# A three-layer graph network on one core: clears and edge work moved behind the first layer's loads, tiles loaded ahead of weight rows, a second weight buffer, an earlier read of the branch register

## What is computed

```python
deg = segment_sum(ones, dst);  deg_inv = 1 / max(deg, 1)
def sage(h, W_self, W_neigh, b):
    mean = segment_sum(h[src], dst) * deg_inv[:, None]
    return h @ W_self + mean @ W_neigh + b
h   = relu(sage(x, W_self0, W_neigh0, b0))
x   = layernorm(x + sage(h, W_self1, W_neigh1, b1))
g   = x @ W.T + b
d   = deg_of_src_with_self_loops ** -0.5
out = layernorm(x + segment_sum(d[row] * d[col] * g[col], row))   # edges and self loops
```

## Time and profile before

| | |
|---|---|
| three timed executions | 949.64, 946.65, 945.94 us, median 946.65 us |
| the profiled execution | 954.31 us, its span 952.6 us |
| PE matmul busy | 880.7 us, 92% of the span |
| PE weight load, DVE, ACT, POOL busy | 747.3, 383.1, 144.4, 411.7 us |
| chain of work that ended last | PE 81%, DMA 7%, DVE 5% |
| mean granted TensorE clock | 0.965 |

### The profile page before, as it was taken

One profiled execution on the slowest core, in us unless ns is written; L12 is line 12 of the kernel. 1 busy time (PEld: TensorE's weight loads), 2 busy tenths in 40 slices (PEclk: granted clock), 3 DMA queues, 4 the chain that ended last, 5 costly groups with the idle time before them and its releaser, 6 DMA issues.

```text
span 952.6 us, 11246 instructions
## 1 busy us (share of the span) xinstructions
PE 880.7 (92%) x4403; PEld 747.3 (78%) x4403; DVE 383.1 (40%) x683; ACT 144.4 (15%) x200; POOL 411.7 (43%) x335
## 2 busy tenths in 40 slices
PE   4749998799997999979997899999999999999996
PEld 3538887688897888968886688888888989988885
DVE  3284667100003676721114122223665643445554
ACT  3101113101102211220104000001111222210000
POOL 3038878877778687786777882000000000000000
PEclk9679999899997999989999799999999999999999
DMA  8926864546376788543347477886656666755551
GB/s 299 383 69 211 306 199 126 164 108 182 100 210 176 188 274 272 161 123 90 90 113 265 146 259 235 276 273 195 198 165 216 202 214 195 270 188 180 200 207 66
DMA packets 109818, 185.56 MB, mean 195 GB/s; under 512 B 16398, under 2 KB 85014, under 8 KB 103616
## 3 DMA queue, kind: packets, MB, share of 16 engines
q1 hardware_dynamic: 58320, 113.56, 36.8%
q10 hardware_dynamic: 40208, 69.37, 20.1%
q0 software_dynamic: 11232, 1.84, 3.5%
HBM read 114.83 MB, written 69.69 MB: 194 GB/s over the span
## 4 chain that ended last, share of the span: by engine, by line
PE 81%; DMA 7%; DVE 5%; another core or an unknown queue 2%; issue 2%; ACT 1%; POOL 0%; ACTq 0%; SPq 0%; DVEq 0%; POOLq 0%
PE ps L1134 41%; PE ps L1209 10%; PE ps L1222 9%; PE ps L1157 9%; PE ps L1189 9%; DMA u<-edges_scr 4%; DMA xs<-xt_scr 2%; PE ps L1120 1%; DVE w L760 1%; PE ps L1178 1%; PE ps L1090 1%; PE ps L1080 1%; ACT outb L631 1%; DVE repeat L825 1%
## 5 line engine op out<-in xcount | busy, mean ns | idle before, releaser
L1134 PE MATMUL ps<-w,xs 128*128 128x512 f32 x1440 | 348.0, 403 | 41.2 <-ACT w L578 16.4
L1134 PEld LDWEIGHTS ps<-w,xs 128*128 128x128 f32 x1440 | 278.6, 195 | 103.0 <-ACT w L578 18.7
L513 POOL DMA_INDIRECT adj_in<-mult,idx_in x160 | 199.5, 1247 | 96.4 <-issue 96.4
L513 POOL DMA_INDIRECT adj_out<-loops,idx_out x160 | 200.8, 1255 | 68.6 <-issue 61.8
L1157 PE MATMUL ps<-xs,w 128*128 128x512 f32 (+1 forms) x576 | 113.6, 358 | 9.2 <-DMA xs<-xt_scr 8.2
L1157 PEld LDWEIGHTS ps<-xs,w 128*128 128x128 f32 x576 | 96.9, 191 | 26.2 <-DMA xs<-xt_scr 8.6
L1189 PE MATMUL ps<-w,u 128*128 128x256 f32 (+3 forms) x640 | 99.3, 314 | 1.2 <-issue 0.9
L1134 PE MATMUL ps<-u,xs 128*128 128x512 f32 x432 | 98.2, 389 | 0.0
L1189 PEld LDWEIGHTS ps<-w,u 128*128 128x128 f32 (+1 forms) x640 | 90.0, 194 | 9.1 <-issue 2.2
L1134 PEld LDWEIGHTS ps<-u,xs 128*128 128x128 f32 x432 | 81.0, 188 | 16.8
L1209 PE MATMUL ps<-u,xs 128*128 128x512 f32 (+1 forms) x400 | 91.3, 390 | 0.2 <-issue 0.2
(11 more groups left out here) (128 smaller groups left out, 581.3 us busy)
## 6 DMA issues: line engine op xcount, KB each, us to landing
xs<-xt_scr SPq DMA_DIRECT2D x30, 1024.0 KB
xt_scr<-xs ACTq DMA_DIRECT2D x10, 1024.0 KB
xin<-in_x SPq DMA_DIRECT2D x18, 512.0 KB
xs<-xt_scr SPq DMA_DIRECT2D x16, 512.0 KB
adj_in<-u ACTq DMA_DIRECT2D x4, 1600.0 KB, 20.9
adj_out<-u ACTq DMA_DIRECT2D x4, 1600.0 KB
w<-adj_in SPq DMA_DIRECT2D x5, 1280.0 KB, 8.1
xs<-adj_in SPq DMA_DIRECT2D x10, 640.0 KB, 5.4
```

Of the source, the lines that this page charges most:

```text
L513: pool.indirect_dma_start(table, bass.IndirectOffsetOnAxis(ap=index[0:EP, j:j + 1], axis=0), counts[0:EP, j:j + 1], None, bounds_check=CEL ...
L1134: ins = nc.tensor.matmul(acc[:, cols], xs[:, t % 2, k, left * T:(left + 1) * T], w_row(q, k, right)[:, cols], start=(i == 0), stop=(i == l ...
```

## The change

The change has six parts. (a) ACT issues the four zero transfers into `adj_in` after all eight splits of N0's weights, not after four. (b) DVE's edge work in N0 is spread: `edge_cells` and `edge_form` move one tile later, `repeats` two tiles later or more, the last two behind S0's splits. (c) PE turns the next tile of x after 4 steps of a tile instead of 16, except in tile 0, and N0's first step waits for the high part of x alone. (d) In S0 and S1, SP issues the first tiles' loads ahead of weight rows 4 to 7. (e) N1 and GCN use a second raw weight buffer (the first 1024 columns of `key`), and the square root of `dsum` moves from the end of mean0 to block 27 of 32. (f) PE reads the flag register after `linear(N0, 3)`; bank 6 comes first in S0's block order.

```diff
-    BLOCK_ORDER = (4, 5, 6, 7, 0, 1, 2, 3)
+    BLOCK_ORDER = (6, 4, 5, 7, 0, 1, 2, 3)
...
-        raw_slots = [raw[:, 0, :], raw[:, 1, :], outb[:, 0, :], outb[:, 1, :]]
+        raw_slots = [raw[:, 0, :], raw[:, 1, :], outb[:, 0, :], outb[:, 1, :], key[:, :, :].rearrange("p g c -> p (g c)")[:, 0:D]]
...
-                raw_slot[l, k] = 0 if l in (N1, GCN) else k % 2 if l == "wt" else k % 4
+                raw_slot[l, k] = k % 2 * 4 if l in (N1, GCN) else k % 2 if l == "wt" else k % 4
...
@@ SP, ahead of S0 @@
-            for k in range(KD):
+            for k in range(4):
                 sp.wait_ge(w_lo_done, KD * S0 + k - 3)
                 load_w(S0, k)
             for i, (c, k) in enumerate(S0_STEPS):
                 t0, n = CHUNKS0[c]
+                if i == 2:
+                    for row in range(4, KD):
+                        sp.wait_ge(w_lo_done, KD * S0 + row - 3)
+                        load_w(S0, row)
...
@@ SP, mean0 @@
-                if m in (0, 4, 8, 12, 16, 28):
-                    k = min(m // 4, 5)
-                    sp.wait_ge(w_lo_done, KD * N1 + k)
+                if m in (0, 1, 4, 8, 12, 16, 30):
+                    k = {0: 0, 1: 1, 4: 2, 8: 3, 12: 4, 16: 5, 30: 6}[m]
+                    if k == 1:
+                        sp.wait_ge(batch_ready, GROUPS)
+                    elif k >= 2:
+                        sp.wait_ge(w_lo_done, KD * N1 + k - 1)
                     load_w(N1, k)
...
-            for k in (6, 7):
-                sp.wait_ge(w_lo_done, KD * N1 + k)
-                load_w(N1, k)
+            sp.wait_ge(w_lo_done, KD * N1 + 6)
+            load_w(N1, 7)
...
@@ SP, ahead of S1 @@
-            for k in range(KD):
-                if k < 4:
-                    sp.wait_ge(w_lo_done, KD * (N1 + 1))
-                else:
-                    sp.wait_ge(w_lo_done, KD * S1 + k - 3)
+            for k in range(4):
+                sp.wait_ge(w_lo_done, KD * (N1 + 1))
                 load_w(S1, k)
...
             for t in range(NT):
                 sp.wait_ge(acc_full, acc_index(S1, t - 2) + 1)
                 load_tile(t)
+                if t == 0:
+                    for k in range(4, KD):
+                        sp.wait_ge(w_lo_done, KD * S1 + k - 3)
+                        load_w(S1, k)
...
@@ SP, gather @@
             load_w(GCN, 0)
+            load_w(GCN, 1)
...
-                for k in {1: (1, 2), 2: (3, 4), 3: (5,)}[c]:
-                    sp.wait_ge(w_lo_done, KD * GCN + k)
+                for k in {1: (2, 3), 2: (4, 5), 3: (6,)}[c]:
+                    sp.wait_ge(w_lo_done, KD * GCN + k - 1)
                     load_w(GCN, k)
...
@@ ACT @@
             for k in range(KD):
                 split_hi(N0, k)
-                if k == 3:
-                    clear(adj_in, cleared_in)
+            clear(adj_in, cleared_in)
             store_turned(0)
...
+                if m == 27:
+                    act.wait_ge(dscale_step, 1)
+                    nc.scalar.activation(dsqrt[:, :], dsum[:, :], ACT.Sqrt).then_inc(dsqrt_done, 1)
             store_h(31)
-            act.wait_ge(dscale_step, 1)
-            nc.scalar.activation(dsqrt[:, :], dsum[:, :], ACT.Sqrt).then_inc(dsqrt_done, 1)
...
@@ DVE, N0 @@
                     turn_lo(t + 1)
                     if t == 0:
                         edge_keys()
+                    elif t == 1:
                         edge_cells()
                     evict_lo(N0, t)
-                    if t == 0:
+                    if t == 1:
                         edge_form()
                         repeats(0)
                         dve.wait_ge(b0_turned, 1)
                         nc.vector.tensor_copy(b0c[:, :], ps[:, 7, 0:KD]).then_inc(b0c_ready, 1)
-                    repeats(t + 1)
+                    elif t >= 2:
+                        repeats(t - 1)
...
+            for g in range(NT - 2, GROUPS):
+                repeats(g)
...
@@ PE @@
                 if q == N0:
-                    pe.wait_ge(xt_lo_done, t + 1)
+                    pe.wait_ge(xt_hi_done, t + 1)
...
-                    if q == N0 and t < NT - 1 and i == 16:
+                    if q == N0 and t < NT - 1 and i == (16 if t == 0 else 4):
                         turn_tile(t + 1)
...
+                    if q == N0 and (k, left) == (0, 1):
+                        pe.wait_ge(xt_lo_done, t + 1)
...
             for t in range(NT):
                 linear(N0, t)
+                if t == 3:
+                    pe.wait_ge(flag_ready, 2)
+                    general = pe.value_load(flag[0:1, 0:1], min_val=0, max_val=1)
...
             self_turned()
-            general = pe.value_load(flag[0:1, 0:1], min_val=0, max_val=1)
             with pe.If(general > 0):
```

More of the change, by code:

```diff
@@ L197, in build @@
         x_full = sems("x_full", 2)
-        raw_full = sems("raw_full", 4)
+        raw_full = sems("raw_full", 5)
         xt_stored = sems("xt_stored", 2)
@@ L264, in build @@
         weights = [w_neigh0, w_self0, w_neigh1, w_self1, wt_scr]
-        raw_slot, raw_count, loads = {}, {}, [0] * 4
+        raw_slot, raw_count, loads = {}, {}, [0] * 5
         for l in (N0, S0, N1, S1, "wt", GCN):
             for k in range(KD):
-                raw_slot[l, k] = 0 if l in (N1, GCN) else k % 2 if l == "wt" else k % 4
+                raw_slot[l, k] = k % 2 * 4 if l in (N1, GCN) else k % 2 if l == "wt" else k % 4
                 loads[raw_slot[l, k]] += 1
@@ L476, in _ @@
                 if t == 1:
-                    for k in (6, 7):
-                        sp.wait_ge(w_lo_done, KD * GCN + k)
-                        load_w(GCN, k)
+                    sp.wait_ge(w_lo_done, KD * GCN + 6)
+                    load_w(GCN, 7)
                     for j in range(4):
@@ L943, in _ @@
                     dve.wait_ge(dsum_done, done)
+                    if done == NT // 2:
+                        nc.vector.tensor_scalar(dsum[:, :], dsum[:, :], 1.0, None, ALU.add).then_inc(dscale_step, 1)
                 if d == 5:
@@ L949, in _ @@
             h_rest(31)
-            nc.vector.tensor_scalar(dsum[:, :], dsum[:, :], 1.0, None, ALU.add).then_inc(dscale_step, 1)
             split_lo(N1, 6)
@@ L1153, in self_turned @@
                             pe.wait_ge(acc_free, acc_index(N0, 8 + d // 2) + 1)
-                        elif first and d == 6:
-                            pe.wait_ge(flag_ready, 2)
                         for left, right in ((0, 0), (0, 1), (1, 0)):
```

## The result

| | before | after |
|---|---|---|
| median of four timed executions | 947.31 us (945.94 to 949.64) | 903.37 us (902.75 to 904.90) |
| ratio after / before | | 0.9522, 95% interval 0.9504 to 0.954 |
| the profiled execution, its span | 954.31, 952.6 us | 903.53, 901.8 us |
| mean granted TensorE clock | 0.965 | 0.985 |
| PE matmul busy | 880.7 us, 92% | 869.2 us, 96% |

The kernel became 44 us faster. That is 18 us short of the 885 us forecast, and above the range's upper end of 900. The waits of PE show where: total us, times, longest, as in the earlier trace rows.

What follows compares the result with a forecast made beforehand. PE is busy nearly throughout, so time returns only from its waits (five hold 56.1 us) and the half clock behind them. Savings of 61.2 us take the profiled 954.3 to 893.1, less 7.7 gives 885 us; range 877 to 900.

Steps and rivals of the forecast that it cites:

- the offset: Whole kernel: the median of timed runs lies 7.7 us below the profiled execution, taking 893.1 to 885 us.
- N0, wait and clock: N0's first tiles: tile 2 starts at 40.5 instead of 66.94, saving 26.4 us of wait and 3.0 of half clock.
- S0, wait: Start of S0: first pieces of x issued one tile earlier remove the wait, 8.1 us.
- S0, clock: Behind S0's first wait: the half clock goes with the wait, 1.9 us.
- wait in front of mean0: Branch to mean0: the early register read gives 2 us of lead, 2.0 us saved, bounds 0.7 and 4.4.
- N1 and S1: First tiles of N1 and S1: waits of 4.8 and 9.8 us go, each with 2.6 us of half clock.
- The rate of 0.22 MB/us: SP's queue beside POOL's before the zeros: three weight rows take 7.1 us, row 7 cast at 22.5.
- rival 1: N0: edge windows land at 45.3, PE waits 11.4 us in tile 1 plus 2.5 of half clock; 899 us, chance 0.17.
- the limit of 33.9: N0, tile 1: windows must land by 33.9 for PE not to wait; expected at 28.5, margin 5.4 us.
- Rival 2: Waits form again one transfer later, as at S0's piece 2 with 2.6 us of margin; 892 us, chance 0.13.
- rival 3: Front of mean0: the moved read gives only its own 0.7 us, the fetch being the wait; 886.5 us, chance 0.2.
- rival 4: mean0: POOL's puts become the bound, each us of start after 70 costing one; 890 us at 75, chance 0.05.

Runs made afterwards that it cites:

- fourth kernel: Changed kernel with tile 0's store ahead of the zeros, zeros paired behind stores of tiles 1 and 2, POOL's windows held until weight row 6 is cast: 902.53 us.
- the fastest kernel: The fourth kernel with zeros behind the stores of tiles 2 and 3, and the other zeros, edge work, `bad` and register read later: 887.38 us.
- twelfth kernel: Changed kernel with the register read back in front of the branch, bank 6 still first: 904.79 us.
- fifth kernel: Changed kernel with the load of mean0's second group of panels moved from the end of S0 to block 4 of mean0: 901.58 us.
- the tenth: The fastest kernel with the load of mean0's second panels held until PE's first matmuls of mean0 are done, ahead of block 4: 889.07 us.

## Why the prediction missed, step by step

The miss has two parts. In the profiled executions the change saved 50.8 us where the sum had 61.2: 10.4 us, and the step that failed is N0's. The other 7.7 us are the offset: I took the profiled execution of before to stand above its median for good. Four medians of that kernel in the study lie between 947.3 and 949.3, and its profiled 954.3 lies above every timed execution (the highest 952.5), while the changed kernel's profiled 903.5 is at its median. The offset belonged to one execution and should have been taken as a bound. The timed executions show 44 us saved, so some 7 of the 50.8 us in the table are this one execution's and not the change's; in which rows they lie isn't shown.

| | predicted | measured |
|---|---|---|
| N0, wait and clock | 29.4 | 14.4 (end at 149.0 against 163.4) |
| S0, wait | 8.1 | 8.1 |
| S0, clock | 1.9 | 2.9 (the stage's length, 111.9 against 114.7) |
| wait in front of mean0 | 2.0 | 2.1 |
| length of mean0 | 0 | 3.3 |
| N1 and S1 | 19.8 | 20.1 |
| sum | 61.2 | 50.8 (954.31 - 903.53; the terms are rounded) |

**N0, the step that failed.** The prediction put row 7 at 22.5, tile 1's start at 28.0, tile 2's at 40.5. The runs gave 27.15, 33.15 and 52.29. Three things are in the 15.0 us:
1. *The store of tile 0*, listed as "(0.3)" of issuing behind the zeros. I costed its instruction and not its landing, and did not ask who waits for it: `store_turned(0)` frees the half of `xs` for the cast of tile 2. The order in the front part shows it directly behind the four transfers. Its landing at 51.1 costs 4.2 us of wait and 3.2 of half clock; moving it alone gave 7.4.
2. *Row 7*, 4.7 us late. The rate of 0.22 MB/us came from a stretch of 2 us, in which POOL's packets took 5.7% of the DMA engines' time. Over 16 to 28 us they took 32.5%, and SP's queue moved less:

```profile
q1 hardware_dynamic: 509, 1.79, 63.5%
q0 software_dynamic: 559, 0.88, 32.5%
```

   1.79 MB in 12 us is 0.15 MB/us, where SP's queue alone moved 0.35 (fourth kernel). The two queues move nearly packet for packet (509 against 559), and POOL's packets are the smaller ones, so the windows take turns from SP for few bytes. Holding them brought row 7 to 18.9; that experiment settles it. I had asked what the rows leave to the windows, and not what the windows take from the rows.
3. *Tile 1*, 2.4 us longer than planned. Some 1.7 of them are lower clock (0.57 granted in the 4 us from 34), behind waits of 2.2 and 0.6 us; the sum had such waits (2 and 0.8 us) but no clock for them. The rest isn't resolved. Another 0.5 us is there because four zeros and the store took 4.8 us to issue instead of 3.4.

**The windows (rival 1)** landed at 30.3: the second transfer was issued at 11.7 and took 18.6 us (transfers of line 518, then their times to landing).

```profile
L518 POOL DMA_DIRECT2D u<-edges_scr x2: 1957/1982/2007, 9.7 to 11.7; - x2
...
DMA to landing us min/median/max: 15.6/17.1/18.6
```

That is 1.8 us after the 28.5 I had said and 3.6 ahead of the limit of 33.9. `key` starts only at 34.37 because DVE's list has tile 1's low part ahead of it, and that waited for ACT's late cast. PE read `bad` at 44.04 without a wait. The fourth kernel shows what late windows cost, 16.9 us of wait, and not how likely they were. The rivals and the range had no case for an ACT transfer behind the zeros, though the method used for SP's queue (what stands behind what) would have found it.

**S0 and S1 (d), N1 (e)** were right in mechanism and size: 10.8, 12.4 and 7.7 us when undone, against 10.0, 12.4 and 7.4. For N1 the 7.7 is the buffer's alone, the square root kept where the change put it. Rival 2 did not come: PE does not wait for piece 2 nor for tile 1.

**mean0 (f).** The branch now starts 2.3 us ahead of PE's last matmul (258.7 against 261.0), the wait is 4.6 and the half clock stays, all as said. But the undone read shows that half of the lead is not the read's: with it in front the lead is still 1.4 us, where the kernel before had 0.4. So the read gives about 0.9 us, rival 3 had the nearer size, and the other 1.2 us (6.7 to 5.5) come from somewhere I did not isolate; the block order is the likely place and was not tried alone. That the sum of both, 2.1 us, is so near the 2.0 said was luck. The branch itself took 6.7 to 7.1 us with the panels under way, 4.6 without them and 3.9 in the fastest kernel, where they are issued just behind its start. The Trainium skill (Runtime: NRT & Kernel Launch, instruction fetch mechanics) says that a taken branch to code outside the fetched window waits until a DMA has brought it. These lengths fit that; no run here moved the code itself.

**mean0's length**, 3.3 us less, was not foreseen. Nearly all of it, 3.1 us, lies in the third chunk: 24.2 us before and 21.1 after. In the kernel before PE's matmuls come haltingly there from 375 to 381: 29 of them in 6 us, where the 11 us before have 89, with 0.9 us of waits and the granted clock at 1.00. The twelfth kernel, whose mean0 is the changed kernel's, loses 2.2 us in the same way in its fourth chunk. So this need not come from the change; the cause stays open.

**The puts (rival 4)** had room: they start at 66.4, 3.6 us before the limit of 70 that the prediction gave. In the fastest kernel PE is 22 us further ahead, and they decide.

**What the parts of N0 gave** is not separated. The parts undone one by one give 10.8 + 12.4 + 7.7 + 2.8 + 1.4 and nothing for (a), 35 of the 44 us. Part (c), the square root's place and the block order were not tried alone. But the remaining 9 us need not be theirs, because (a) and (b) can stand in for each other: in the kernel before PE waits 12.6 us for DVE in front of tile 2. With (b) undone alone 2.1 us of such a wait come back, with (a) undone alone none, though `key` starts at 45.8 again. The two undone together were not run.

## What to carry to other kernels

When a large transfer is moved in an engine's list, look at every transfer that now stands behind it in the same queue and ask who waits for its landing, not for its issue; a small store behind 6.55 MB cost as much here as the whole move had won. Read a queue's rate over a stretch as long as the one it is used for, and count what a queue of small packets takes from one of large packets, in both directions. Undo parts that guard against the same wait together as well as one by one. And before time is won ahead of a stage, see whether the stage has an input with a clock of its own.

## What the runs showed of the hardware

- A 1 MB store issued behind four zero transfers of 1.64 MB each from the same engine landed 20.2 us after issue; issued ahead of them it landed after 6.3 us.
- Queues of different engines shared the DMA engines nearly packet for packet: 509 of SP's with 1.79 MB against 559 of POOL's with 0.88 MB in 12 us. With POOL's windows held, the last row was cast at 18.9 instead of 28.1.
- The windows needed about 20 us beside the weight rows (issued from 9.7, landed at 30.3) and without them (issued from 20.0, `key` at 40.2), and 35 us in the kernel before, with the zeros under way (issued from 9.8, `key` at 45.3).
- PE's branch took 6.7 to 7.1 us with the 2.6 MB of panels under way, 4.6 without them, and 3.9 in the fastest kernel, where they are issued 0.4 us after it begins; the second branch took 3.3 before, 3.7 after and up to 4.5 in the fourth kernel.
- Two waits of 2.5 us in front of mean0 differ in what came behind them: the granted clock stayed at 1.00 in the fifth kernel and was 0.77 and 0.67 in the 6 us from 243 in the tenth. Behind 4.6 us it was 0.50 for 3 us.
